# Carries added in a counted loop of 28-column pieces, and source rows scattered four columns per group, in a four-layer graph network on one core

## What is computed

```python
def step(f, _):                                        # layer 0, ten times
    f = f * src_norm[:, None]
    f = jax.ops.segment_sum(f[src], dst, num_segments=n) * dst_norm[:, None]
    return (1.0 - ALPHA) * f + ALPHA * feat0
...
e = leaky_relu(a_src[:, src] + a_dst[:, dst] + fc_b[0])  # layer 1, four heads: softmax over the edges of a source
out = segment_sum(att * hp[:, dst], src).mean(heads) + bias
...
msg = jnp.einsum('eb,ebo->eo', w_comp[etype], jnp.einsum('ei,bio->ebo', x[src], weight))   # layer 2
a = tanh(relu(sum((x[src] @ A1.T + b1) * (x[dst] @ A2.T + b2 + rel_emb[etype])) / sqrt(32)))
nei = segment_sum(a[:, None] * msg, dst); h = relu(where(in_deg > 0, nei + h[src[last_e]] @ self_loop, 0))
...
aggr = segment_sum(node_feat[src] * edge_attr[:, None], dst) + node_feat               # layer 3
```

## Time and profile before

| | |
|---|---|
| median of 3 executions | 2836.77 us (2835.66 to 2837.78) |
| profiled execution | 2836.26 us |
| its span in the trace | 2834.5 us |
| DVE busy | 2001.7 us (71%) |
| POOL busy | 1726.3 us (61%) |
| ACT busy | 621.8 us (22%) |
| PE busy | 536.7 us (19%) |
| mean granted clock of PE | 0.573 of full speed |

### The profile page before, as it was taken

The page is one execution under the profiler, slowest core; times in us unless marked ns, Lnnn a source line. Parts: engine busy times, 40 slices in busy tenths (PEclk is TensorE's granted clock), DMA queues, the critical chain, the costliest instruction groups (busy, mean ns, idle before and its releaser), DMA issues.

```text
span 2834.5 us, 24933 instructions
## 1 busy us (share of the span) xinstructions
PE 536.7 (19%) x3578; PEld 340.6 (12%) x3578; DVE 2001.7 (71%) x3750; ACT 621.8 (22%) x1382; POOL 1726.3 (61%) x1741
## 2 busy tenths in 40 slices
PE   5760000471000000000003032320355450000000
PEld 3330000371000000000003011210122220000000
DVE  7777888788735555528998574279778788678772
ACT  7972333130000000000003023431333430100000
POOL 6777767777466665544757776650465550707776
PEclk9995555796555555555556565555555555555555
DMA  6003332100121122212121101110000001110000
GB/s 222 13 12 99 99 94 83 31 13 12 57 13 30 19 20 24 28 10 103 24 64 21 60 10 10 59 60 0 5 7 6 7 8 46 23 3 10 9 9 9
DMA packets 100895, 101.69 MB, mean 36 GB/s; under 512 B 58169, under 2 KB 92649, under 8 KB 98929
## 3 DMA queue, kind: packets, MB, share of 16 engines
q0 software_dynamic: 53664, 20.91, 8.1%
q1 hardware_dynamic: 46864, 80.15, 7.9%
q10 hardware_dynamic: 320, 0.20, 0.0%
HBM read 38.06 MB, written 60.81 MB: 35 GB/s over the span
## 4 chain that ended last, share of the span: by engine, by line
DVE 41%; issue 18%; POOL 12%; DMA 8%; PE 6%; ACT 3%; DVEq 3%; ACTq 1%; POOLq 0%; SPq 0%
POOL ring L780 3%; POOL cring L475 3%; POOL out_dram L491 2%; DVE YW L1258 2%; DMA cring<-sums_by_list,cidx 2%; DVE RB L1258 1%; PE banks L2701 1%; POOL attention_by_edge L880 1%; POOL ring L873 1%; DVE banks L1089 1%; DVE banks L1099 1%; DVE SW L1095 1%; DVE SW L1094 1%; DVE SW L1104 1%; DVE SW L1389 1%
## 5 line engine op out<-in xcount | busy, mean ns | idle before, releaser
L491 POOL DMA_INDIRECT out_dram<-ring,ridx x196 | 210.5, 1074 | 128.6 <-DVE ridx L2181 68.5
L500 POOL DMA_INDIRECT XS<-in_x_dram,xsi x196 | 199.7, 1019 | 70.2 <-issue 62.3
L500 POOL DMA_INDIRECT SW<-node_table,srci x196 | 200.3, 1022 | 66.1 <-issue 66.1
L500 POOL DMA_INDIRECT XD<-in_x_dram,xdi x196 | 196.1, 1001 | 62.7 <-issue 62.7
L899 POOL DMA_INDIRECT out_dram<-z4w,oidx x98 | 96.3, 982 | 223.9 <-ACT oidx L2455 194.2
L475 POOL DMA_INDIRECT cring<-sums_by_list,cidx x128 | 123.6, 966 | 106.7 <-issue 76.3
L2570 PE MATMUL banks<-tl,dcar 128*128 128x32 f32 (+1 forms) x14 | 4.4, 404 | 779.4 <-DVEq L1371 596.4
L2488 PE MATMUL banks<-YW 128*128 128x392 f16 x784 | 140.3, 333 | 45.3 <-ACT YW L2265 45.3
L780 POOL DMA_INDIRECT ring<-x_by_edge,aidx x96 | 101.0, 1052 | 58.9 <-issue 28.5
L2240 ACT ACT_TABLE_LOAD x22 | 28.2, 1283 | 411.6 <-DVEq L1059 411.6
L1002 DVE TENSOR_SCALAR YW<-YW,b_d 128x784 f16<-128x784 f16 x196 | 82.7, 422 | 46.8 <-PE banks L2488 44.8
(11 more groups left out here) (602 smaller groups left out, 3438.6 us busy)
## 6 DMA issues: line engine op xcount, KB each, us to landing
SW<-in_x_dram SPq DMA_DIRECT2D x20, 625.0 KB
out_dram<-SW SPq DMA_DIRECT2D x20, 625.0 KB
sums_by_list<-RB SPq DMA_DIRECT2D x2, 1800.0 KB
sums_by_edge<-RB SPq DMA_DIRECT2D x1, 3528.0 KB, 9.8
sums_by_list<-RB SPq DMA_DIRECT2D x2, 1600.0 KB
XS<-in_x_dram,xsi POOLq DMA_INDIRECT x196
list_values_by_edge<-RB SPq DMA_DIRECT2D x1, 3136.0 KB
attention_by_edge<-RB SPq DMA_DIRECT2D x1, 3136.0 KB
```

Of the source, the lines that this page charges most:

```text
L491: pool.indirect_dma_start(out=table, out_offset=off, in_=ring_row(h, j, w), in_offset=None, bounds_check=limit, oob_is_err=False).then_inc ...
L500: pool.indirect_dma_start(out=dest[:, t * w:(t + 1) * w], out_offset=None, in_=table, in_offset=bass.IndirectOffsetOnAxis(ap=idx[:, t:t + ...
```

## The change

`carry_run` adds the carry in pieces of RC0 = 28 columns. A piece is two operations on 128 x 896: flags times carry into a scratch tile, and an addition. The loop has as many trips as the longest run needs that crosses a partition's border; with `last=True` it starts from the last piece, for spreads. The count is computed once, in a prelude ahead of L1695, from the flags, the equal trailing columns and the largest number of edges of a source, with a maximum over partitions through PE and a load of the count into a register. By my count on the drawn arrays the longest crossing run has 17 edges on one side of a border and no source has more than 4 edges; (17 + 13.5) / 28 is rounded to 1 trip.

`carry_run` takes the place of the 32 wide operations in S1, S3, S4, S5 and S6, of the 8-column loop in `list_carry` (8 executions) and of `add_first` in the sorted sum, where one operation on the last column comes with it. The copies of the flags (`pfirst`) and of the carry (`car`) go.

Source rows are filled and scattered per group: four fills and an index copy of four columns. The seven slots of the first round are filled inside the norm of `XS`, one after each chunk; the others behind the copy of the transposes in each group of the first six rounds. They wait for the landing of the scatters of three sets of slots. POOL issues 4 scatters per slot, 196 in all as before. A few semaphores are merged, which moves no instruction, and one more row transpose on PE serves the prelude.

```diff
@@ segment_sums @@
                 st.do(V.tensor_copy(pmask[:, 0:T], mask[:, :]))
-                st.do(V.tensor_copy(pfirst[:, 0:T], first[:, :]))
+                if not enter:
+                    st.do(V.tensor_copy(pfirst[:, 0:T], first[:, :]))
@@ list_carry @@
-                pr8 = prod[:, 0:2 * CU * D].rearrange("p (j w) -> p j w", w=D)
-                with cs.trip_loop(2) as i:
-                    ...
-                    cs.seq(V.tensor_tensor(pr8, f, mid(bank[7][:, 0:D], 2 * CU), ALU.mult))
-                    dve.sem_inc(tick, 1)
-                    cs.seq(V.tensor_tensor(zz, zz, pr8, ALU.add))
-                    dve.sem_inc(tick, 1)
+                carry_run(z, lfirst, zw)
@@ ahead of L1695 @@
+            st.do(V.tensor_reduce(runs[:, 0:1], dbak[:, :], AX.X, ALU.max))
+            st.do(V.tensor_reduce(runs[:, 1:2], dfirst[:, :], AX.X, ALU.add))
+            st.do(V.tensor_scalar(t1[:, :], dstf[:, :], dstf[:, T - 1:T], None, ALU.is_equal))
+            st.do(V.scalar_tensor_tensor(out=t2[:, :], in0=srcf[:, :], scalar=float(N), in1=NS3[:, :, 3], op0=ALU.is_lt,
+                                         op1=ALU.mult))
+            ...
+            column_max(car[:, 0:1])
+            st.seq(V.tensor_scalar(runs[:, 0:1], car[:, 0:1], (RC0 - 1) / 2, 1.0 / RC0, ALU.add, ALU.mult))
+            st.seq(V.tensor_scalar(runs[:, 0:1], runs[:, 0:1], MAGIC, None, ALU.add))
+            st.seq(V.tensor_scalar(trips_i[5][:, :], runs[:, 0:1], -MAGIC, 1.0, ALU.add, ALU.max))
+            rn = Steps(dve, s_run, dve.value_load(trips_i[5][0:1, 0:1], min_val=1, max_val=ROUNDS))
+
+            def carry_run(flat, flags, w=D, last=False):
+
+                with rn.trip_loop(2) as i:
+                    at_ = i * -RC0 + (T - RC0) if last else i * RC0
+                    e = prods[:, :, :].rearrange("p a b -> p (a b)")[:, 0:RC0 * D].rearrange("p (t d) -> p t d", d=D)
+                    rows = flat[:, bass.ds(at_ * w, RC0 * w)].rearrange("p (t d) -> p t d", d=w)[:, :, 0:D]
+                    rn.seq(V.tensor_tensor(e, flags[:, bass.ds(at_, RC0)].unsqueeze(2).to_broadcast([P, RC0, D]),
+                                           mid(bank[7][:, 0:D], RC0), ALU.mult))
+                    dve.sem_inc(tick, 1)
+                    rn.seq(V.tensor_tensor(rows, rows, e, ALU.add))
+                    dve.sem_inc(tick, 1)
@@ S1, S3 (and S6 on Y), S4, S5 @@
-            segment_sums(Y3, S3, D, dmask, dfirst)
+            sums_of_dst(Y3, S3, S)
-                spread_back(S3, D, dend, dstf)
+                spread_of_dst()
@@ POOL @@
-            def out_src_slot(n, b):
+            def out_src_group(k, m, j):
...
-                pool.wait_ge(s_oslot, n + 1)
-                for t in range(U):
+                pool.wait_ge(s_oslot, k * RG + (j + 1))
+                for t in range(GT):
@@ ACT @@
+            def out_src_fill(g, j):
+
+                for t in range(GT):
+                    A.activation(oring_row(j, t), XS[:, bass.ds(g * (GT * D) + t * D, D)], ACT.Copy,
+                                 scale=rr[:, bass.ds(g * GT + t, 1)])
+                A.activation(oidx[:, j * GT:(j + 1) * GT], osi[:, bass.ds(g * GT, GT)], ACT.Copy).then_inc(s_oslot, 1)
...
-            norm_acts(XS, sq_2, both=True)
+            norm_acts(XS, sq_2, first_slots, both=True)
...
                 A.activation(xt[:, b, :], bank[4 + b][:, 256:256 + P], ACT.Copy).then_inc(s_xtc[1], 1)
+                if slot_next:
+                    slot_next()
                 act.wait_ge(s_xyu, done(g))
```

More of the change, by code:

```diff
@@ L915, in _ @@
             pool.wait_ge(s_heldw, 16)
-            for b in range(2):
-                pool.wait_ge(s_oland[b], 16 * U * ROUNDS)
+            for m, of_slot in enumerate(SLOT_GROUPS):
+                pool.wait_ge(s_oland[m], 16 * GT * len(of_slot) * ROUNDS)
             for h in range(2):
@@ L1694, in _ @@
             segment_ends(dmask, dcar, dend)
+            st.do(V.tensor_reduce(runs[:, 0:1], dbak[:, :], AX.X, ALU.max))
[3 more added lines that the diff above has]
+                                         op1=ALU.mult))
+            st.wait()
+            st.do(V.tensor_reduce(runs[:, 2:3], t1[:, :], AX.X, ALU.add))
@@ new lines, in _ @@
+            st.do(V.tensor_reduce(runs[:, 3:4], t2[:, :], AX.X, ALU.max))
+            st.do(V.tensor_tensor(runs[:, 1:2], runs[:, 1:2], runs[:, 0:1], ALU.mult))
+            st.wait()
+            st.seq(V.scalar_tensor_tensor(out=runs[:, 2:3], in0=runs[:, 2:3], scalar=tm[:, 0:1], in1=runs[:, 3:4],
+                                          op0=ALU.mult, op1=ALU.max))
+            st.seq(V.tensor_tensor(tl[:, 0:1], runs[:, 1:2], runs[:, 2:3], ALU.max))
+            column_max(car[:, 0:1])
+            st.seq(V.tensor_scalar(runs[:, 0:1], car[:, 0:1], (RC0 - 1) / 2, 1.0 / RC0, ALU.add, ALU.mult))
@@ L1695, in _ @@
+            sums_of_dst = lambda src3, dst3, flat: segment_sums(src3, dst3, D, dmask, dfirst,
+                                                                enter=lambda first: carry_run(flat, first))
+            spread_of_dst = lambda: spread_back(S3, D, dend, dstf, enter=lambda flags: carry_run(S, flags, last=True))
             st.seq(V.tensor_scalar(t2[:, :], NS3[:, :, 1], 0.0, None, ALU.is_equal))
@@ L1748, in _ @@
             dve.sem_inc(s_ltab[0], 1)
-            dve.sem_inc(s_pay, 1)
+            dve.sem_inc(s_full, 1)
             def fill0(i, h):
@@ L2023, in add_first, with enter_sorted @@
                     dve.sem_inc(tick, 1)
-            segment_sums(SA3, SA3, D, smask, sfirst, T=CW, enter=add_first)
+            def enter_sorted(first):
+                carry_run(SA, first)
+                st.seq(V.scalar_tensor_tensor(out=SA3[:, CW - 1, :], in0=bank[7][:, 0:D], scalar=first[:, CW - 1:CW],
+                                              in1=SA3[:, CW - 1, :], op0=ALU.mult, op1=ALU.add))
+            segment_sums(SA3, SA3, D, smask, sfirst, T=CW, enter=enter_sorted)
             spread_back(SA3, D, send, ks, T=CW, t1=t1c, t2=t2c, enter=add_first)
@@ L2433, in _, with relation_group @@
             stage(1, XD3, 0, 0)
-            def relation_group(g, j, last):
+            def relation_group(g, j, last, slot_next=None):
                 b = j % 2
@@ L2501, in _ @@
             M.matmul(bank[4][:, 0:2 * HA_CH], up[:, :], tk, start=True, stop=True)
-            M.matmul(bank[5][:, 0:2 * HA_CH], ones[:, :], tk, start=True, stop=True).then_inc(s_base, 1)
+            M.matmul(bank[5][:, 0:2 * HA_CH], ones[:, :], tk, start=True, stop=True).then_inc(s_hist, 1)
             pe.wait_ge(s_nt, 1)
@@ L2573, in _ @@
             key_rows(3)
-            carry(dcar, D)
             column_row(4)
@@ L2577, in _ @@
             column_row(5)
+            carry(dcar, D)
+            column_row(6)
             carry(dcar, 1)
             carry(dbak, 1)
-            column_row(6)
+            column_row(7)
             carry(dcar, D)
@@ L2618, in _ @@
             pe.wait_ge(s_sgo, SINGLES)
-            key_rows(7)
-            pe.wait_ge(s_trw, 8)
+            key_rows(8)
+            pe.wait_ge(s_trw, 9)
             for h in range(NH):
```

74 lines of the change are left out of this document (37 added, 37 removed).

## The result

The changed kernel takes 2749.44 us (median of 4, 2746.28 to 2749.9) against 2837.11 us before (median of 4, 2835.66 to 2837.78): ratio 0.9689, 95% interval 0.9672 to 0.9706. The forecast was 2749, its range 2733 to 2772. The profiled execution took 2749.16 us, its span is 2747.4 us, 87.1 less than before.

The account below looks back on a forecast made before the run. DVE led the last chain with 41% of the span, but its savings count only where DVE is waited for. Carries, spread and relation stage savings less the prelude sum to -87.7 us: 2836.8 to 2749, 80% range 2733 to 2772.

Parts of the forecast that it names:

- Three wide carries at 12.2: In the segmented sums S1, S3 and spread S6, 32 additions become one multiplication and one addition: 12.2 us saved each.
- S4 at 7.1 of 12.1: Spread behind S3: DVE 12.1 us earlier, but SP's row moves let the write of `x` move only 7.1 us.
- Nothing from the sorted sum and S5: Layer 1: savings of about 6 and 12 us vanish into DVE's waits at L1396 and L1491; 0 and 0.
- Lists: Carries of the passes over lists: 8.4 us saved on list 0, seven times 0.3 or 2.1 us on list 1.
- POOL's cover: POOL's 9.42 us idle for DVE behind list 0 shrinks to 1.0, so the 8.4 us saving is just realised.
- Relation stage, 39.1: Blocks of 28 fills leave seven places: 5.5 us at the start, 5.6 at each of six round ends; bounds 36 and 41.
- Prelude, 5.6: New DVE operations ahead of S1, computing the trip count with nothing hiding them: cost 5.6 us, bounds 5 and 6.5.
- Fills on the chain: Rival: ACT lacks spare time ahead of the self-loop copy, 42 groups grow 1.0 us each: 2791 us; chance 0.14, whole or part.
- More trips: Rival: carry loops need more trips, 2.96 us each; two trips add 33 us, 2782; two or three trips have chance 0.06.
- the run of edges that leads there: Slower case, chance 0.03: gain used up between three and four trips, decided from a crossing run of 99 columns.
- All DVE time realised: Rival: S4 gives 5 us more, waits at L1396 and L1491 hide nothing, 6 + 12 more: 2726 us; chance 0.08.
- The forecast's own range: 2741 to 2757 us, from the bounds of S4, the prelude and the stage added crosswise; chance 0.64.

## Why the prediction was right

*Three wide carries at 12.2.* S1, S3 and S6 were worth 12.4, 12.4 and 12.2. The form that no row of before showed came out at its assumed price: 14 multiplications and 14 additions, each 1.09 us (one addition 1.15), the one that reads PE's result no longer than the other. The run with S1 undone confirms it. By the cost in the Trainium skill ("VectorE: DVE Perf Modes", section "The TRN2 errata") a wide carry would have saved 6 us. This case's runs don't agree: the removed operations took 14.68 / 32 = 0.46 us each and not 0.26. The same section of the Trainium skill adds that its 58 cycles are too few, and gives (N + 151) / 0.96 ns for an fp32 addition of N elements. By estimates from that, 896 elements take 1.09 us, which the new operations did, and 196 take 0.36, still short of the 0.46. What the rest is no run here shows; the removed operations read and wrote every 32nd word of the sums.

*S4 at 7.1 of 12.1.* The trace shows 7.2, and the runs show why: with S4 undone SP waits for DVE, and with the write out of SP's queue the edit moves POOL's gathers by 10.2 us. The wait for moved rows that I expected at L1257's successor is there, 3.08 us.

*Nothing from the sorted sum and S5.* The waits grew from 83.2 to 88.0 and from 14.0 to 26.9; the run that undoes both is as fast.

*Lists.* List 0 gave 8.4, with POOL's cover down to 1.09 us as forecast: of any further saving there no more than about 1.1 us could be realised. List 1 gave 2.6 with what lies between, against 2.1.

*Relation stage, 39.1.* The mechanism was right and the size was not: 35.9 in the traces, just under my lower bound of 36, and 34.9 by the run. The start was worth 5.3 (forecast 5.5), the six round ends 5.1 each and not 5.6. I had counted on the idle 5.16 and a wait of 0.5 for products going whole. The wait of 0.5 went, at the multiplication behind a round's first product. But of the 5.16 only 4.8 went: the first product now waits 0.36 for the bias addition just ahead of it, which the long idle had covered. And the first round's groups took 0.3 more. The multiplication behind the first product of round two, in the timeline of DVE before and after:

```profile
2059.26 1.23 DVE L2086 TENSOR_TENSOR prods<-banks,RB 128x1024 f32<-128x1024 f32 x1 [0.53 <-PE banks L2701]
```

```profile
2009.20 1.23 DVE L2122 TENSOR_TENSOR prods<-banks,RB 128x1024 f32<-128x1024 f32 x1
```

*Prelude, 5.6.* Mis-sized the other way: 4.6 in the trace, since the load of the count took 0.67 and not 1.17 and the operations stood closer together than I had added up. So the sum was better than its terms: 1.0 us more gain than forecast here, 1.6 in the carries and between them, and 0.9 ahead of any change (the trace with S1 undone was only 0.1 early there, with the same code up to there, so this looks like chance) stand against 3.2 less in the relation stage, 0.7 behind S6 and 0.2 between. That the median met the forecast to 0.4 us is therefore in part luck.

*The rivals.* Fills on the chain: not below 3.5 us more per group. More trips: their price was right within the 6 us that the runs can tell, and the change turns into a loss between three and four trips, as forecast. But the run of edges that leads there was reckoned wrong: (85 + 13.5) / 28 is already rounded to 4, so it is 85 columns and not 99. All DVE time realised: no.

*The forecast's own range.* The bounds of S4, the prelude and the stage, added crosswise, give 2742 to 2755; its upper end of 2757 is 2 us more than they do.

## What to carry to other kernels

Ask at every place of an edit who waits next and in which queue: of the eight places where the carry was made shorter here, five gave their full length (S1, S3, S6 and both lists), S4 gave seven twelfths because another engine's queue held an earlier job, and two gave nothing. Taking the held job to an idle engine's queue gave back 2.3 of the 5.0 us here, since the transfers that then ran side by side held each other up. Work that an engine does in a block at a round's end can be free in pieces, if each piece fits the idle time that the engine has in every step; measure that idle by adding work until the time moves. A loop whose trip count depends on the data is cheap only as long as the data keep it short: price a trip and say at what count it loses.

## What the runs showed of the hardware that I had not expected

A large write held up small transfers that other engines had issued about the same time. The write of `x` is 3.2 MB. Issued from ACT at 1387.71, while POOL's last gather of rows was still under way, it took 11.8 us to land, against 9.1 on SP's queue, where that gather had landed before, and the gather, issued 0.4 us ahead of it, 8.5 us against 4.7. SP's second row move, which waits for the gather, left 3.4 us later. On SP's queue the write did the same to what stood behind it: the 2 KB of indices issued 1.2 us after it took 8.1 us to land, and 2.8 with the write on ACT, where most of it was through by then.

POOL's scatters, 0.98 us each in the relation stage, took up to 1.89 us while the norm of `XS` ran on DVE beside them (the mean of the `z4w` scatters is 1.016 us over all 112, before 0.982 over 98). It cost nothing, since POOL had idle time there (4.56 us ahead of the first scatter of `e4w`).
